# Cross attention of a decoder layer by groups of four heads: scores on row strips, a pass for the maximum and a turned pass

## The chip, the cores and the metric

The kernel runs on one core of one Trainium2 chip. The metric is the time of one execution in device microseconds. The core has a matrix engine (TensorE, PE in the rows; its weight loads are PEld), a vector engine (VectorE, DVE), a scalar engine (ScalarE, ACT), GpSimd (POOL) and a queue that issues the transfers (SyncE, SP). Each takes its instructions in the order in which they are written, and they wait for one another by semaphores.

## What is computed

One decoder layer over 16 batches of 100 rows of width 512, with a context of 722 rows of width 384 for each batch. 16 heads of 32 columns.

```
x = x + self_attention(layernorm(x))            # causal, with rotation of q and k
x = x + cross_attention(layernorm(x), context)
x = x + experts(layernorm(x))                   # 8 experts, two per row, softmax gates

def cross_attention(x, cond):
    q = (x @ q_w + q_b), k, v = split(cond @ kv_w + kv_b)     # 16 heads of 32
    attn = softmax(q k^T / sqrt(32))                          # 100 x 722 a head
    return (attn v) @ proj_w + proj_b
```

## The kernel before

Matrix products run in fp16 with each operand split in a high and a low half: `split3` adds three products (high by high, high by low, low by high).

**Stages.** A prologue transposes and splits the weights. Then `pipeline` runs iterations n = -1 to 16. Iteration n does the cross attention of batch n (`cross`), the preparation of batch n+1 (`prep`: its self attention, and q, k and v of its cross attention) and the output projection of batch n-1 (`tail`, chunks TT and TP). Iterations 1 to 12 are a hardware loop with four in its body; the others are written out. Iteration -1 has only preparation; iteration 15 has no preparation, and does the first tiles of the expert layer's input (chunks FG, FW, FX, FL) instead; iteration 16 has only the tail and the late FX tiles. Then `experts` runs 8 experts over 13 tiles of 128 rows.

**Order.** An iteration has 16 steps, one per head. `STEP_CHUNKS` gives each step its chunks of preparation: X1T and X2T transpose a normalised x, SQ, SK, SV and CQ are products of it, CX0 to CX5 transpose the context, CK0 to CK7 and CV0 to CV5 make keys and values, SS0 to SS3 and SP0 to SP3 are scores and transposed probabilities of self attention, SO and OP its output and projection. The chunks rotate through four PSUM banks; PE makes a chunk, ACT its high half, DVE its low half, and `bank_free` lets chunk c start when chunk c-4 is out. `PE_ORDER = "0SOT123"` is PE's order within a step: the step's first chunk, scores of the next head (S), output of the head before (O), transposes of this head's probabilities (T), the other chunks. `ACT_ORDER` and `DVE_ORDER` do the same for those queues. POOL runs rotation of q and k, the subtraction and scaling of the self attention's softmax, the layer norms and the scaling of the heads, in the order of `pool_iteration`.

**Cross attention of a head.** `pe_scores` (L743) multiplies a stack of q (high, low, high on 96 partitions) by a stack of k (high, high, low): two matmuls of 361 columns give the scores with the 100 rows of x on the partitions. The stacks are made by 24 DMAs an iteration from `split_k` and `split_qk` (L577, L582). `dve_max` takes the maximum over 722 columns (L989) and a bias from it (L992). `act_exp` (L853) writes the exponentials and their sum. `pe_transpose_probs` (L765) transposes them in fp32, six matmuls, `act_probs_high` (L859) copies the high half, `dve_probs_low` (L997) subtracts it. `pe_head_out` (L754) adds 12 matmuls of 64 columns. After four heads DVE joins the halves (`dve_heads_sum`), and once per batch POOL scales by the inverse sums.

Of the kernel before, what the change touches and what calls it, by code (L numbers as in the profile page):

```python
# [21 lines left out]
F32 = mybir.dt.float32  # L22
F16 = mybir.dt.float16
# [4 lines left out]
P = 128  # L28
# [8 lines left out]
CW = 121  # L37
LCP = CT * CW
HC = LC // 2
HP = LCP // 2  # L40
TT = (T + P - 1) // P
# [7 lines left out]
OCOL = 304  # L49
# [9 lines left out]
    ["CX1", "SK"],  # L59
    ["CX2", "CX3", "SV"],  # L60
    ["CX4", "CX5", "TT"],
    ["SS0", "SS1", "TP"],
    ["SS2", "SS3", "CK0"],
    ["CV0", "CK1"],
    ["SP0", "SP1", "CK2"],
    ["SP2", "SP3", "CK3"],
    ["CK4", "SO"],
    ["CK5", "OP"],
    ["CK6", "CK7"],
    ["X2T", "CV1", "CQ"],  # L70
    ["CV2", "CV3"],
    ["CV4"],
# [6 lines left out]
EARLY = 11  # L79
EXTRA_CHUNKS = {  # L80
    B - 1: {0: ["FG0", "FW0"], 1: ["FW1"], 2: ["FW2", "FW3"], **{t + 3: [f"FX{t}"] for t in range(EARLY)},
            15: ["FL0"]},

    -1: {3: ["BV0", "BV1"]},
# [3 lines left out]
PE_ORDER = "0SOT123"  # L88
ACT_ORDER = "0PE123"
# [3 lines left out]
    [f"CX{c}" for c in range(6)] + ["FG0"] + [f"FW{k}" for k in range(KD)] + [f"FX{t}" for t in range(TT)] + [f"CK{c}" for c in range(8)] + [f"CV{c}" for c in range(6)])  # L93


class Iteration:


    def __init__(self, n, odd, cross=True, prep=True, tail=True):
        self.n, self.odd, self.cross, self.prep, self.tail = n, odd, cross, prep, tail  # L100
        self.steps = [[c for c in step if (tail if c in ("TT", "TP") else prep)] for step in STEP_CHUNKS]
# [4 lines left out]

    @staticmethod
    def _count(names):
        return len(names), sum(c in SPLIT for c in names)

    def _before(self, which):
        every = [c for step in STEP_CHUNKS for c in step]
        head = self._count([c for c in every if c not in ("TT", "TP")])[which]
        each = self._count(every)[which]
        prep = head
        head += self._count([c for step in EXTRA_CHUNKS[-1].values() for c in step])[which]
        if isinstance(self.n, int):
            last = ["TT", "TP"] + [c for step in EXTRA_CHUNKS[B - 1].values() for c in step]
            return 0 if self.n < 0 else head if self.n == 0 else (
                head + prep + (min(self.n, B - 1) - 1) * each + (self.n - B + 1 > 0) * self._count(last)[which])  # L120
        return head + prep + (self.n - 1) * each
# [28 lines left out]
def build_layer(nc, x, ctx, sWq, sbq, sWk, sbk, sWv, sbv, sWo, sbo, cWq, cbq, cWkv, cbkv, cWp, cbp,  # L150
                gW, gb, eW, eb, rope, x2_dram, out):
    with ExitStack() as stack:
# [16 lines left out]
        b_rows = sb("b_rows", [6 * KD, P])  # L169
# [6 lines left out]
        x_mid = [sb(f"x_mid{i}", [L, D]) for i in range(2)]  # L176
# [1074 lines left out]
```

## Time and profile before

| what | us |
|---|---|
| three runs | 1566.31, 1567.98, 1581.59; median 1567.98 |
| profiled execution | 1573.9 |
| its span, first to last instruction | 1572.1, mean granted clock 0.955 |
| prologue and iteration -1, up to the first cross scores | 92.6 |
| iterations 0 to 14 | 92.6 to 1175.5 |
| iterations 15 and 16, up to the experts | 89.0 |
| experts | 307.6 |

The page gives the busy time of each engine. The windows view gives it for any stretch, with the granted clock of TensorE. The timeline lists instructions in order of time, runs of equal ones merged: "x12" with one duration is a block of twelve, and the distance from its start to the next row's start is what it takes when the queue is full. A value in brackets is the idle time before, with what ended it.

### The profile page before, as it was taken

How to read it: one execution, taken by the hardware profiler on the slowest of the kernel's cores; microseconds unless marked ns; L12 is line 12 of the kernel's file. 1: busy time of each engine (PE TensorE's matmuls, PEld its weight loads, DVE VectorE, ACT ScalarE, POOL GpSimd, SP SyncE). 2: the span in 40 equal slices, each digit the busy share in tenths (PEclk: the TensorE clock that was granted, in tenths of full speed). 3: DMA queues.
4: the chain of work that ended last, by engine and by line, in shares of the span. 5: the costliest groups of instructions: out<-in, count | busy, mean ns of one | idle time of the engine just before them, and what ended most of it. 6: DMA issues, size and time to landing. Idle time of an engine off the chain costs nothing.

```text
span 1572.1 us, 36339 instructions
## 1 busy us (share of the span) xinstructions
PE 1445.6 (92%) x14004; PEld 1025.8 (65%) x14004; DVE 1069.9 (68%) x1926; ACT 689.2 (44%) x1336; POOL 372.2 (24%) x490
## 2 busy tenths in 40 slices
PE   4889999999989999998999999999996789999999
PEld 4467777777676777776777767677765644444444
DVE  4658878787868687787878686878877554333332
ACT  4336555565646455555556465646554310000000
POOL 1522313133222323141313223232313100000000
PEclk8999999999999999999999999999997589999999
DMA  7133140404132231404040413223133010000002
GB/s 246 28 73 78 28 97 9 99 8 99 40 68 49 57 70 42 94 12 100 8 99 7 99 25 81 49 57 84 28 64 135 1 43 27 28 27 27 28 0 84
DMA packets 82917, 90.38 MB, mean 57 GB/s; under 512 B 32429, under 2 KB 68581, under 8 KB 82749
## 3 DMA queue, kind: packets, MB, share of 16 engines
q1 hardware_dynamic: 82748, 88.05, 23.2%
q8 instruction: 117, 1.92, 0.5%
q14 instruction: 52, 0.42, 0.1%
HBM read 41.06 MB, written 6.55 MB: 30 GB/s over the span
## 4 chain that ended last, share of the span: by engine, by line
PE 64%; DVE 15%; issue 7%; ACT 5%; POOL 4%; SPq 2%; DMA 1%; DVEq 0%; POOLq 0%; ACTq 0%
PE psum L258 43%; PE psum L765 7%; PE psum L743 4%; DVE c_max L989 4%; PE psum L754 3%; DVE s_sum L1051 2%; DVE c_raw L939 2%; ACT prob L853 1%; POOL c_raw L1193 1%; PE psum L697 1%; DVE probT L997 1%; SPq L577 1%; POOL x_norm L1138 1%; PE psum L673 1%; DVE stats L1019 1%
## 5 line engine op out<-in xcount | busy, mean ns | idle before, releaser
L859 ACT ACTIVATE probT<-psum 121x600 f16<-121x600 f32 x256 | 171.8, 671 | 262.1 <-PE psum L765 261.5
L989 DVE TENSOR_REDUCE c_max<-psum 100x1 f32<-100x722 f32 x256 | 231.8, 905 | 78.0 <-PE psum L743 72.6
L853 ACT ACTIVATE prob<-psum,c_bias 100x722 f32<-100x722 f32 x256 | 220.0, 859 | 40.7 <-DVE c_bias L992 40.2
L765 PE MATMUL psum<-ident,prob 100*121 100x100 f32 x1536 | 233.1, 291 | 0.0
L997 DVE TENSOR_TENSOR probT<-psum,probT 121x600 f16<-121x600 f32 x256 | 199.3, 778 | 26.3 <-ACT probT L859 21.5
L258 PE MATMUL psum<-w_kv,cT 128*121 128x512 f16 x864 | 199.4, 379 | 0.0
L765 PEld LDWEIGHTS psum<-ident,prob 100*121 100x121 f32 x1536 | 195.8, 197 | 0.1
L258 PE MATMUL psum<-cT,w_kv 128*128 128x361 f16 x1152 | 195.8, 317 | 0.0
L481 DVE SCALAR_TENSOR_TENSOR w_self_all<-psum,g_now,w_self_all 128x512 f32<-128x512 f32 x104 | 77.8, 751 | 167.5 <-PE psum L258 167.5
L743 PE MATMUL psum<-arena,stack_q 96*100 96x361 f16 x512 | 130.6, 338 | 33.2 <-ACT prob L853 30.3
L258 PEld LDWEIGHTS psum<-w_kv,cT 128*121 128x121 f16 x864 | 112.6, 134 | 59.0
L258 PEld LDWEIGHTS psum<-cT,w_kv 128*128 128x128 f16 x1152 | 110.6, 98 | 57.9
L754 PEld LDWEIGHTS psum<-cv,probT 121*128 121x128 f16 x3072 | 129.7, 100 | 28.5 <-DVE probT L997 3.9
L754 PE MATMUL psum<-cv,probT 121*128 121x64 f16 x3072 | 137.8, 196 | 2.0 <-DVE probT L997 1.6
L258 PE MATMUL psum<-w_cross_q,arena 128*128 128x512 f16 x528 | 118.9, 383 | 1.0 <-DVE w_self_all L481 1.0
L258 PE MATMUL psum<-w_cross_p,arena 128*128 128x512 f16 x528 | 116.1, 379 | 0.0
L848 ACT ACTIVATE cv<-psum 121x512 f16<-121x512 f32 x96 | 57.3, 597 | 106.6 <-PE psum L258 106.2
L839 ACT ACTIVATE split_k<-psum,b_part 128x361 f16<-128x361 f32 x128 | 72.0, 562 | 69.4 <-PE psum L258 68.2
L743 PEld LDWEIGHTS psum<-arena,stack_q 96*100 96x100 f16 x512 | 56.3, 129 | 62.6 <-ACT prob L853 41.4
L1133 POOL TENSOR_SCALAR shift<-moments 100x1 f32<-100x1 f32 x32 | 7.5, 235 | 366.2 <-DVE moments L1021 366.2
L258 PEld LDWEIGHTS psum<-w_cross_q,arena 128*128 128x128 f16 x528 | 51.7, 99 | 64.0 <-issue 5.3
L920 DVE TENSOR_TENSOR cv<-psum,cv 121x512 f16<-121x512 f32 (+1 forms) x98 | 67.6, 690 | 37.5 <-ACT cv L848 33.3
(160 smaller groups left out, 2091.5 us busy)
## 6 DMA issues: line engine op xcount, KB each, us to landing
arena<-split_k SPq DMA_DIRECT2D x192, 180.5 KB, 3.9
c_raw<-in_ctx SPq DMA_DIRECT2D x16, 907.5 KB
stack_q<-split_qk SPq DMA_DIRECT2D x192, 25.0 KB, 1.9
split_k<-in_L_ffn_expert_w SPq DMA_DIRECT2D x4, 1024.0 KB, 5.1
cv<-in_L_ffn_expert_w SPq DMA_DIRECT2D x4, 1024.0 KB, 5.1
x_in<-in_x SPq DMA_DIRECT2D x16, 200.0 KB
x_scratch<-x_mid SPq DMA_DIRECT2D x16, 200.0 KB
w_self_all<-x_scratch SPq DMA_DIRECT2D x12, 256.0 KB, 6.0
```

Of the source, the lines that this page charges most:

```text
L258: last = pe.matmul(out_ap, a(pa), b(pb), start=(i == 0 and j == 0), stop=(i == len(pairs) - 1 and j == 2))
L481: dve.scalar_tensor_tensor(y[:, t], psum[:, (t + odd) % 4, 0:D], g_now[:, odd, t:t + 1], y[:, t], ALU.mult, ALU.add).then_inc(y_done, 1)
L743: last = pe.matmul(score[0:L, hf, 0:HC], stack_q[odd][:, h], stack_k[odd][:, h, hf * HC:(hf + 1) * HC], start=True, stop=True)
L754: last = pe.matmul(pT[:, h % 4 // 2, o:o + 2 * DH], probT_all[:, c:c + P], cv[odd][:, t, h].rearrange("k p d -> k (p d)"), start=t + p == ...
L765: last = pe.transpose(pT[0:CW, t // 3, (t % 3) * L:(t % 3 + 1) * L], prob[h % 2][:, t * CW:(t + 1) * CW], ident[0:L, 0:L])
L839: op = act.activation(split_k[:, 0, i // 2, (i % 2) * HC:(i % 2 + 1) * HC], f[:, 0:HC], ACT.Identity, bias=b_part[:, 3, i // 2:i // 2 + 1])
L848: op = act.activation(cv[not it.odd][:, i, :, 0], f[0:CW, 0:D].rearrange("k (h d) -> k h d", h=H), ACT.Copy)
L853: act.activation(prob[h % 2][:, 0:LC].rearrange("q (a k) -> q a k", a=2), score[0:L, :, 0:HC], ACT.Exp, bias=c_bias[:, int(odd), h:h + 1], ...
L859: act.activation(probT[:, 0].rearrange("k (a c) -> k a c", a=2), pT[0:CW, :, 0:3 * L], ACT.Copy)\
L920: return dve.tensor_tensor(dst, src, high, ALU.subtract)
L989: dve.tensor_reduce(c_max[:, int(odd), h:h + 1], score[0:L, :, 0:HC], AXIS.XY, ALU.max)\
L997: return dve.tensor_tensor(probT[:, 1].rearrange("k (a c) -> k a c", a=2), pT[0:CW, :, 0:3 * L], probT[:, 0].rearrange("k (a c) -> k a c", ...
```

## The change

Four heads (a group, k = 0 to 3) share their steps. c is the step within the group. Head h of a group lives on partitions 32c to 32c+31 of q and k, and these are used where they lie: the stacks and their 24 DMAs are gone.

- `pe_scores(o, hf)`: for one half (361 keys) of a group, three rounds (high by high, high by low, low by high) of four matmuls, one per strip of 32 rows, into banks 0 to 3. DVE takes the maxima of four heads at once (1444 columns), twice per group, and joins the two halves.
- Chunk MX transposes the maxima and splits them in a high and a low half on two rows of each strip.
- `pe_turned_scores(o, part)`: keys on the partitions (128 to a tile, three tiles to a part, two parts), 100 rows of x as columns. Four rounds of four strips for each tile, the fourth a matmul that subtracts the maxima. ACT writes the exponentials of 1200 columns to `prob`, then copies the high half to `prob16`; the low half is subtracted by POOL for groups 0 to 2 and by DVE for group 3. No transposes of probabilities.
- `pe_head_out`: as before, with a column of ones in v that gives the sum; 65 columns. It runs two groups behind.
- The scores use banks 0 to 3 and chunks 4 to 7; each of the four steps of a group fills the same banks 0 to 3 again.
- POOL's list is written out by step; chunks are put on other steps; TP writes to a buffer of its own; the gate weights and rows for the experts are loaded an iteration earlier; three late tiles instead of two.

```diff
-CW = 121
+CW = 128
+PT = 3 * HT * L
 STEP_CHUNKS = [
     ["X1T", "CX0", "SQ"],
...
+    ["CX1", "CX2", "SK"],
+    ["MX0", "CX3", "CX4", "CX5"],
+    ["SV", "CK0"],
+    ["CK1", "SS0", "SS1"],
+    ["CK2", "SS2", "SS3"],
+    ["MX1", "CK3", "CK4"],
+    ["CK5", "CK6"],
+    ["SP0", "SP1", "CV0"],
+    ["SP2", "SP3", "TT", "CV1"],
+    ["SO", "MX2", "TP"],
+    ["OP"],
+    ["CK7", "CV2"],
+    ["X2T", "CV3", "CQ"],
+    ["MX3", "CV4"],
     ["CV5"],
 ]
-EARLY = 11
+EARLY = 10
-    -1: {3: ["BV0", "BV1"]},
+    -1: {6: ["BV0", "BV1"]},
-PE_ORDER = "0SOT123"
-ACT_ORDER = "0PE123"
+PE_ORDER = "0S123"
+ACT_ORDER = "0E1H23"
 DVE_ORDER = "M0L123"
...
+        def pe_scores(pe, n, odd, o, hf):
+            for i, (a, b) in enumerate(((0, 0), (0, 1), (1, 0))):
+                for c in range(HT):
+                    rows = slice(DH * c, DH * (c + 1))
+                    last = pe.matmul(score[0:L, c, 0:HC], cq[odd][rows, a, o],
+                                     split_k[odd][rows, b, o, hf * HC:(hf + 1) * HC], start=i == 0, stop=i == 2)
+            last.then_inc(score_ready, 1)
+        def pe_turned_scores(pe, odd, o, part):
+            for j in range(3):
+                t = 3 * part + j
+                for i, (a, b) in enumerate(((0, 0), (0, 1), (1, 0), (None, None))):
+                    for c in range(HT):
+                        rows = slice(DH * c, DH * (c + 1))
+                        last = pe.matmul(score[:, c, j * L:(j + 1) * L],
+                                         minus[rows] if a is None else split_k[odd][rows, b, o, t * CW:(t + 1) * CW],
+                                         max_split[rows, o % 2] if a is None else cq[odd][rows, a, o],
+                                         start=i == 0, stop=i == 3)
+            last.then_inc(turned_ready, 1)
+        def pe_head_out(pe, n, odd, o, c):
+            if c == 0:
+                if o == GROUPS - 1:
+                    pe.wait_ge(prob_low_last, 2 * n + 2)
+                else:
+                    pe.wait_ge(prob_low, 2 * (GROUPS - 1) * n + 2 * o + 2)
...
+        def pe_cross(pe, it, h):
+            n, k, c = it.n, h // HT, h % HT
+            g = GROUPS * n + k
...
+            if c == 0 and it.cross:
+                pe.wait_ge(max_done, 2 * g + 1)
+            if c == 0 and (begun or (it.cross and k == 3)) and (it.cross or k < 2):
+                pe.wait_ge(heads_summed, g - 2)
+            if c == 1 and it.cross:
+                pe.wait_ge(max_done, 2 * g + 2)
+            if c >= 2 and (begun or (it.cross and k > 0)) and (it.cross or k == 0):
+                pe.wait_ge(exp_done, 2 * g - 3 + c)
+            if k >= 2 and it.cross:
+                pe_head_out(pe, n, it.odd, k - 2, c)
+            elif k < 2 and begun:
+                pe_head_out(pe, n - 1, not it.odd, k + 2, c)
+            if c == 0 and it.cross:
+                pe_scores(pe, n, it.odd, k, 1)
+            elif c in (1, 2):
...
+            elif c == 3:
...
+        def act_exp(act, n, o, part):
...
+            act.activation(prob[:, part].rearrange("k (c q) -> k c q", c=HT), score[:, :, 0:3 * L], ACT.Exp, scale=SOFT)\
+               .then_inc(exp_done, 1)
+        def act_probs_high(act, n, o, part):
...
+            act.activation(prob16[o % 2][:, part * PT:(part + 1) * PT], prob[:, part], ACT.Copy).then_inc(prob_high, 1)
+        def dve_max(dve, n, o, hf):
+            g = GROUPS * n + o
+            dve.wait_ge(score_ready, 2 * g + hf + 1)
+            dve.tensor_reduce(c_most[:, hf], score[0:L, :, 0:HC], AXIS.X, ALU.max).then_inc(max_done, 1)
...
+        def dve_cross(dve, it, h):
+            if c == 0 and it.cross:
+                dve_max(dve, n, k, 1)
+                dve_join_max(dve, n, k)
+            if c == 3:
...
         for what in DVE_ORDER:
             if what == "M":
+                dve_cross(dve, it, h)
             elif what == "L":
+                if h in (2, 3) and begun:
+                    dve_probs_low(dve, n - 1, h - 2)
+                if h in SUM_STEPS and it.prep:
+                    dve_self_sums(dve, m, SUM_STEPS.index(h))
...
         def pool_iteration(pool, it):
+            for h in range(H):
+                if it.prep:
+                    if h == 0 and not (isinstance(n, int) and n < 0):
+                        pool_bias(pool, x_in[:], 2 * m, b_so)
+                    if h in (1, 2):
+                        for part in range(3):
+                            pool_rotate(pool, it, h - 1, part)
+                    if h in (5, 6):
+                        for g in (2 * h - 10, 2 * h - 9):
+                            pool_self_shift(pool, m, g)
+                    if h == 12:
+                        pool_norm(pool, x_mid[not it.odd][:], 2 * m + 1)
+                    if h == 13:
+                        pool_bias(pool, x_mid[not it.odd][:], 2 * m + 1, b_cp)
+                    if h == 14:
+                        pool_split_q(pool, not it.odd, m)
+                    if h == 15 and more:
+                        pool_norm(pool, x_in[:], 2 * m + 2)
+                if h == 8 and begun:
+                    pool_heads_scale(pool, n)
+                if it.cross and h // HT > 0 and h % HT in (2, 3):
+                    pool_probs_low(pool, n, h // HT - 1, h % HT - 2)
+                if it.prep and h in (7, 8):
+                    for g in (2 * h - 14, 2 * h - 13):
+                        pool_self_scale(pool, m, g)
```

## Rows read from the trace of the kernel before

**Rows 1.** The page's first part: busy time, share of the span, instructions.
```profile
PE 1445.6 (92%) x14004; PEld 1025.8 (65%) x14004; DVE 1069.9 (68%) x1926; ACT 689.2 (44%) x1336; POOL 372.2 (24%) x490
```

**Rows 2.** Windows: stretch, length, busy time of each engine, PEclk, DMA share, GB/s.
```profile
162.30:1175.50 1013.20, 954.51 (x10754) 737.02 (x10753) 797.50 (x1442) 563.63 (x1106) 298.66 (x378) 0.98 0.26 56
162.30:233.30 71.00, 67.03 (x770) 51.26 (x769) 57.17 (x104) 40.27 (x79) 21.34 (x27) 1.00 0.27 59
1175.50:1264.50 89.00, 63.74 (x580) 51.93 (x579) 52.55 (x100) 34.14 (x68) 21.68 (x46) 0.64 0.18 62
1264.50:1572.10 307.60, 300.26 (x1432) 141.84 (x1430) 118.84 (x200) 20.23 (x36) 3.56 (x8) 0.99 0.10 34
```

**Rows 3.** PE timeline, iteration end and start: start, us, instruction, [idle before].
```profile
379.55 0.56 PE L630 MATMUL psum<-ident,x_norm 100*128 100x100 f32 x4 [1.56 <-POOL x_norm L1138]
...
382.24 2.31 PE L258 MATMUL psum<-xT,w_self_all 128*128 128x100 f16 x48 [0.46 <-DVE xT L920]
...
384.71 0.47 PE L743 MATMUL psum<-arena,stack_q 96*100 96x361 f16 x2
385.02 0.51 PE L754 MATMUL psum<-cv,probT 121*128 121x64 f16 x12
385.37 0.85 PE L765 MATMUL psum<-ident,prob 100*121 100x100 f32 x6
386.06 1.14 PE L258 MATMUL psum<-xT,w_self_all 128*128 128x100 f16 x22
```

**Rows 4.** PE timeline: a block of 361 columns, then one on row strips.
```profile
331.68 1.55 PE L258 MATMUL psum<-cT,w_kv 128*128 128x361 f16 x9
333.07 2.10 PE L258 MATMUL psum<-w_kv,cT 128*121 128x512 f16 x9
...
395.93 0.76 PE L665 MATMUL psum<-split_qk 32*100 32x100 f16 x24 [0.65 <-DVE cT L920]
396.62 0.36 PE L743 MATMUL psum<-arena,stack_q 96*100 96x361 f16 x1
```

**Rows 5.** Groups by form: shapes, count, busy us, mean ns, idle before.
```profile
L989 DVE TENSOR_REDUCE c_max<-psum 100x1 f32<-100x722 f32 x256 | 231.8, 905 | 78.0 <-PE psum L743 72.6 <-issue 0.8
L853 ACT ACTIVATE prob<-psum,c_bias 100x722 f32<-100x722 f32 x256 | 220.0, 859 | 40.7 <-DVE c_bias L992 40.2
...
L997 DVE TENSOR_TENSOR probT<-psum,probT 121x600 f16<-121x600 f32 x256 | 199.3, 778 | 26.3 <-ACT probT L859 21.5
...
L1051 DVE TENSOR_REDUCE s_sum<-c_raw 100x8 f32<-100x800 f32 x32 | 31.4, 981 | 2.6 <-ACT c_raw L889 2.4
...
L1169 POOL TENSOR_TENSOR split_qk<-tmp_q,split_qk 128x400 f16<-128x400 f32 x16 | 15.1, 946 | 1.3
...
L907 DVE SCALAR_TENSOR_TENSOR w_kv<-cv,w_kv 128x3072 f16<-128x3072 f32 x1 | 3.3, 3348 | 0.0
...
L871 ACT ACTIVATE w_kv<-cv 128x3072 f16<-128x3072 f32 x1 | 2.8, 2767 | 0.0
```

**Rows 6.** Timeline of all engines before X1T: the norm's first step.
```profile
376.11 0.68 DVE L1019 BATCH_NORM_STATS2 stats<-x_in 100x6 f32<-100x512 f32 x1
```

**Rows 7.** Windows: 3 us around a hole and 3 us after.
```profile
304.40:307.40 3.00, 1.49 (x21) 1.23 (x20) 2.44 (x6) 2.07 (x4) 1.79 (x4) 1.00 0.25 46
307.90:310.90 3.00, 3.00 (x24) 2.75 (x23) 1.59 (x3) 0.60 (x2) 0.85 (x1) 0.50 0.12 21
```

**Rows 8.** PE timeline: prologue's end, a back edge, start of the last iteration.
```profile
92.62 0.79 PE L743 MATMUL psum<-arena,stack_q 96*100 96x361 f16 x2 [2.60 <-DMA stack_q<-split_qk]
...
453.58 0.92 PE L630 MATMUL psum<-ident,x_norm 100*128 100x100 f32 x4 [4.50 <-issue]
...
1184.63 0.56 PE L710 MATMUL psum<-ident,x_in 8*128 8x8 f32 x4 [7.62 <-DMA x_in<-in_L_ffn_gate_w]
```

**Rows 9.** POOL timeline: the norms of the late tiles.
```profile
1273.45 0.77 POOL L521 TENSOR_SCALAR w_self_all<-w_self_all,nmean,rstd 128x512 f32<-128x512 f32 x1
...
1275.58 0.77 POOL L521 TENSOR_SCALAR w_self_all<-w_self_all,nmean,rstd 128x512 f32<-128x512 f32 x1
```

More of the change, by code:

```diff
@@ L100, in __init__ @@
         self.n, self.odd, self.cross, self.prep, self.tail = n, odd, cross, prep, tail
-        self.steps = [[c for c in step if (tail if c in ("TT", "TP") else prep)] for step in STEP_CHUNKS]
+        self.steps = [[c for c in step if self._has(c)] for step in STEP_CHUNKS]
         if isinstance(n, int):
@@ L105, in __init__, with _has, _count @@
         self.order = [c for step in self.steps for c in step]
+    def _has(self, name):
+        return self.tail if name in ("TT", "TP") else self.cross if name[:2] == "MX" else self.prep
     @staticmethod
-    def _count(names):
-        return len(names), sum(c in SPLIT for c in names)
+    def _count(names, which):
+        return sum(c in SPLIT for c in names) if which else len(names)
     def _before(self, which):
         every = [c for step in STEP_CHUNKS for c in step]
[L113 to L116, printed above, removed]
+        late = self._count([c for c in every if c in ("TT", "TP")], which)
+        first = self._count([c for step in EXTRA_CHUNKS[-1].values() for c in step], which)
+        first += self._count([c for c in every if c not in ("TT", "TP") and c[:2] != "MX"], which)
+        each = self._count(every, which)
         if isinstance(self.n, int):
[L118 to L121, printed above, removed]
+            last = self._count([c for c in every if c in ("TT", "TP") or c[:2] == "MX"], which)
+            last += self._count([c for step in EXTRA_CHUNKS[B - 1].values() for c in step], which)
+            return 0 if self.n < 0 else first if self.n == 0 else (
+                first + each - late + (min(self.n, B - 1) - 1) * each + (self.n - B + 1 > 0) * last)
+        return first - late + self.n * each
     def bank(self, chunk):
@@ L183, in build_layer @@
         split_qk = sb("split_qk", [P, 4, KD, L], F16)
[L184 removed]
+        cq_all = sb("cq", [P, 2, 2, KD, L], F16)
+        cq = [cq_all[:, i] for i in range(2)]
         sv = sb("sv", [L, H, 2, DH], F16)
@@ L1171, in pool_iteration @@
-            if isinstance(n, int) and n < 0:
-                pool.wait_ge(chunk_out, it.done("BV1"))
-                pool_bias(pool, x_in[:], 0, b_so)
-            if begun:
-                pool.wait_ge(c_rinv_done, n)
-                pool.wait_ge(pT_out, H * n + 1) if it.cross else pool.wait_ge(c_summed, 1)
-                heads = c_out[:].rearrange("q (h d) -> q h d", h=H)
-                pool.tensor_tensor(heads, heads, c_rinv[:].unsqueeze(2).to_broadcast([L, H, DH]), ALU.mult)\
-                    .then_inc(c_out_done, 1)
```

510 lines of the change are left out of this document (257 added, 253 removed).

## The prediction

> **What bounds the kernel now.** I read the page's first part: TensorE (PE) is busy 92% of the span, VectorE (DVE) 68%, GpSimd (POOL) 24% [rows 1]. Then the windows by stage [rows 2]. The program is a prologue up to the first scores at 92.6 us, sixteen iterations (each: cross attention of one batch, preparation of the next), then the expert layer. The 14 iterations n=1 to 14 take 1013.2 us, 72.4 each, PE busy over 94% of them; iteration 1, at clock 1.00, takes 71.0. The last iteration with what follows it takes 89.0 us at a granted clock of 0.64, and the experts 307.6. The PE timeline shows the price of one head: scores 0.31 us, head output 0.35, transposes 0.69 from start to start [rows 3]. Adding up such starts for a whole iteration gives 65.5 us of issue and some 5.5 of holes (4.0 by the busy record; a last matmul's tail of about 0.2 us hides the rest). The largest hole is where X1T waits for the layer norm, 1.56 us, and SQ for xT, 0.46 [rows 3]. So the loop is bound by PE, and what matters is PE's work and its holes.
>
> **PE's work per iteration.** Removed: 16 x (0.31 + 0.35 + 0.69) = 21.6 us. Added:
> - Head outputs stay, 65 columns instead of 64: 16 x 0.36 = 5.8.
> - Maximum pass: 8 half passes (two per group of four heads), each 12 matmuls of 361 columns on four row strips. The block of 24 matmuls of 100 columns on two strips takes 0.69 us from its start to the next [rows 4], where 24 one behind another, 100 columns each at 2.4 GHz, would need 1.0. So strips run side by side: the starts within the block are about 47 ns apart a round, and 0.13 us is lost at the block's ends. A 361-column matmul is 0.155 us (nine in 1.39 [rows 4]); three rounds and the ends give 0.60 (bounds: 0.60, or 12 x 0.155 = 1.9 if strips took turns). Times 8: 4.8.
> - Turned pass: 8 parts of 12 rounds of 100 columns: 0.56 + 0.13 = 0.69. The stationary has 128 columns; the block has 100. I take 0.75. Upper bound: the head output's 128-column loads come every 29 ns, and four in turn make a round 116 ns and a part 1.52. Times 8: 6.0.
> - MX, four transposes: 0.5.
>
> Sum 17.1, so 4.5 us less per iteration. The 24 stack DMAs go; in the loop PE is seldom late for them.
>
> The Trainium skill ("TensorE: Matmul & The Clock Gate", Measured speedup vs the span model) gives 3.07 times for four row tiles rather than nearly 4; an estimate by it is 0.61 us for a half pass before its ends and 0.7 for a part, some 2 us more per iteration, or 30 us in all. No run here shows four row strips; the two-strip block speaks for the larger gain.
>
> **The new passes as a chain.** Scores of a half, or of a turned part, fill banks 0 to 3, and each step of PE waits until the previous filling was read: by a DVE maximum over 1444 columns (722 take 0.905 and 800 take 0.981, 1.03 ns a column: 1.65 us), or by an ACT exponential over 1200 (1.18, from 0.859 at 722 and the copies of 3072 in 2.77) [rows 5]. Then ACT copies the high half (1.18), and the low half is subtracted: for groups 0 to 2 on POOL (400 columns take 0.946, so 1200 take 2.0 if a third of that was fixed cost and 2.8 if none; I take 2.5), for group 3 on DVE (3072 take 3.35: 1.40) [rows 5]. DVE loses 16 x (0.905 + 0.778) and 16 bias products, and gains 8 x 1.65, 2 x 1.4 and small ones: about 10 us less, ACT 8 less, POOL 15 more (21.3 to 37). None is full. But they are late. I walked one iteration in the order of the four queues, with these durations and 0.05 to 0.2 us from engine to engine. Holes of PE:
> - *Step 0, 6.4 us.* The stats of x_in follow CV4 on DVE; 3.44 us after their start X1T may run [rows 3, 6], 1.9 us after step 15's scores ended. At step 15 POOL runs this norm before the low half of group 2, part 1: 2.5 us more, and PE's first head output of step 0 waits for that (`prob_low`). Then output and scores 0.96, then DVE, whose order puts the maximum (0.2 + 1.65), the join 0.15 and only then X1T's low half 0.57: SQ starts 8.1 us after step 15's scores, and PE has 1.65 us of work for that time. Before: 2.0 us of hole.
> - *Step 4, 1.6.* Output of group 3 waits for the second DVE low half, which stands behind maximum, head sum and SV.
> - *Steps 5 and 6, 0.6.* DVE is full from step 3 to 6.
> - *Step 8, 2.4.* SP0 waits for POOL: shifts of groups 2 and 3 (their maxima late by the DVE queue), two low halves (5.0), then the scaling 0.85.
> - *Step 12, 0.5; step 13, 1.6* (X2T after OP, which stands behind a DVE maximum).
>
> Sum 13.1, against 5.5: +7.6. Without the clock an iteration is 71.0 - 4.5 + 7.6 = 74.1.
>
> **The clock.** The stretch in which PE was busy half the time is followed by one at 0.50, its lower level 1.2 GHz [rows 7]. Over the 14 iterations that and the back edges of the loop (a gap of 4.5 us that the profile puts to issue, once in four iterations [rows 8]) cost 72.4 - 71.0 = 1.4 each. The hole at step 0 (20% busy over 8 us) should bring it down in every iteration, with some 5 us of PE's work inside the slow time: 2.6. So +1.2; the back edges stay. What a slow stay costs at step 8 as well (another 1) I leave to the range. Loop: 14 x (3.1 + 1.2) = +60.
>
> **Ends.** Prologue: PE waits 2.60 us for the stacks before the first scores [rows 8]; with the bias products moved behind CK work I take -4 (bounds -1 and -6). Iteration 0 has no outputs and no turned part in steps 0 to 3, nor a late low half: -3. Last iteration: PE waits 7.62 us for the gate weights at its start [rows 8], which now land an iteration earlier. Against that, each group is a serial chain of two maxima and two exponentials with PE's work at half clock between them, 14 to 16 us against 17.7 for four heads, and group 3 has its turned pass, low half and outputs still to do in the next iteration, some 16 us. Together about 82 against 89: -7 (bounds -25, +5). Experts: three late tiles instead of two; one costs POOL 2.1 us, and PE waits on it [rows 9]: +2.5.
>
> Sum: +60 - 4 - 3 - 7 + 2.5 = +48. The profiled execution took 1573.9 (span 1572.1 and 1.8 around it) and would become 1622; the median shown is 1568.0, so 1616.
>
> **Rivals.**
> 1. *PE stays the bound; the holes don't open* (faster). DVE, ACT and POOL all have room on average (68%, 44%, 24%), and if the low half of group 2 and the scaling are ready in time, the 4.5 us are saved: 14 x -4.5 - 11 = -74, 1494; half of the holes gives about 1530. It decides at the `prob_low` wait: it holds if the POOL subtraction takes well under 1.5 us, or H of step 14 and the subtraction end before the stats. Against it: POOL's 0.946 us for 400 columns hardly varies. 18%.
> 2. *No net change.* Consecutive DVE rows overlap by up to 0.09 us and POOL's 1200 columns may take 2.0; holes 10 instead of 13, clock as before: 14 x 0.1 - 11, 1558, with some loss of clock 1570. 15%.
> 3. *Holes as worked out, clock as before*: 14 x 3.1 - 11.5 = +32, 1600. 12%.
> 4. *The strips don't run side by side in the turned pass*, because 128-column loads take turns: 1.52 a part, +6 an iteration, 5 of it seen: 1616 + 70 = 1686. 10%.
>
> **How the numbers follow.** The forecast (the holes and the clock) has 45%, with 1590 to 1645 as its own range. Slower by over 1% (about what a measurement of this kernel tells from no change): cases 3, 4 and the forecast, 0.67. Within 1%: 0.15. Faster: 0.18. The range 1545 to 1680 takes in case 2, half of the road to case 1, and most of case 4.
>
> **What would show it.** Right: PE busy below 86% in the loop; X1T to SQ over 5 us in each iteration, with POOL's low half of 1200 columns (about 2.5 us) as the releaser at step 0; clock 0.95 or less over the loop; SP0 waiting for the POOL scaling; c_most 1.65 us and the exponential 1.18; the block of a half pass 0.6 and a turned part 0.7 to 0.8 from start to start; the loop at 75 to 78 us an iteration. Wrong: iterations of 68 to 70 us; low halves done before X1T; a turned part of 1.5.

## The result and the profile after

The changed kernel takes 1629.69 us (median of four runs, 1628.57 to 1631.01); the kernel before, beside it, 1571.51. The ratio is 1.035, 95% interval 1.031 to 1.040: slower, by 58 us, where 1616 and 48 were predicted. The span of the profiled execution is 1628.7 us, 56.6 more than before.

The page's first part, to be read against [rows 1]:

```profile
PE 1412.9 (87%) x19700; PEld 919.9 (56%) x19700; DVE 907.5 (56%) x1495; ACT 607.6 (37%) x888; POOL 621.8 (38%) x610
```

PE, DVE and ACT all do less; only POOL does more. PE's busy time fell by 32.7 us and its idle time grew from 126.5 to 215.8. So the time went into waits. The windows by stage (columns as in [rows 2]: the 14 iterations; a stretch within one of them; the last iteration; the experts):

```profile
153.80:1231.40 1077.60, 932.39 (x15739) 649.27 (x15736) 655.34 (x1062) 490.70 (x715) 516.74 (x463) 0.93 0.07 23
620.10:630.30 10.20, 7.50 (x81) 6.40 (x82) 3.33 (x5) 0.49 (x1) 2.22 (x2) 0.50 0.01 2
1231.40:1318.90 87.50, 56.86 (x1084) 44.22 (x1082) 43.22 (x75) 33.15 (x42) 37.56 (x49) 0.65 0.09 28
1318.90:1628.70 309.80, 301.56 (x1448) 142.65 (x1446) 120.24 (x203) 20.80 (x37) 5.35 (x12) 0.99 0.10 34
```

The loop went from 1013.2 to 1077.6 us, 76.97 an iteration, at a clock of 0.93 instead of 0.98. The prologue ends at 85.0 (92.6 before), iteration 0 takes 68.8 (69.7), the last 87.5 (89.0), the experts 309.8 (307.6). The differences are -7.6, -0.9, +64.4, -1.5 and +2.2, together the 56.6 of the span.

Where an iteration loses it, on PE's timeline (one iteration, from 616 us; the brackets hold the idle time before the row and its releaser):

```profile
616.25 0.67 PE L742 MATMUL psum<-arena,cq 32*100 32x361 f16 x12
618.72 0.56 PE L627 MATMUL psum<-ident,x_norm 100*128 100x100 f32 x4 [1.80 <-POOL x_norm L1204]
621.15 0.84 PE L770 MATMUL psum<-cv,arena 128*128 128x65 f16 x12 [1.86 <-POOL arena L1256]
621.92 1.15 PE L742 MATMUL psum<-arena,cq 32*100 32x361 f16 x12
623.00 0.90 PE L699 MATMUL psum<-ident,c_raw 128*128 128x128 f32 x3
625.55 4.18 PE L273 MATMUL psum<-xT,w_self_all 128*128 128x100 f16 x48 [1.66 <-DVE xT L971]
...
643.91 0.53 PE L770 MATMUL psum<-cv,arena 128*128 128x65 f16 x12 [1.30 <-DVE arena L1062]
...
658.96 0.55 PE L670 MATMUL psum<-ident,c_raw 100*100 100x100 f32 x4 [1.72 <-POOL c_raw L1243]
...
677.62 0.54 PE L770 MATMUL psum<-cv,arena 128*128 128x65 f16 x12 [0.88 <-DVE c_rinv L1071]
...
681.62 0.53 PE L627 MATMUL psum<-ident,x_norm 100*128 100x100 f32 x4 [0.82 <-POOL x_norm L1204]
```

From step 15's scores (616.25) to the self projection (625.55) pass 9.3 us, three waits included, one behind the other: for the norm, for the low half, for xT. Four smaller ones follow at steps 4, 8, 12 and 13. The two engines that PE waits for, in the same stretch; first POOL:

```profile
617.90 0.77 POOL L1204 TENSOR_SCALAR x_norm<-x_in,shift,rstd 100x512 f32<-100x512 f32 x1 [0.22 <-POOL rstd L1202]
618.63 2.46 POOL L1256 TENSOR_TENSOR arena<-prob,arena 128x1200 f16<-128x1200 f32 x1
```

then DVE:

```profile
623.12 1.66 DVE L1050 TENSOR_REDUCE c_most<-psum 100x4 f32<-100x1444 f32 x1 [3.49 <-PE psum L742]
624.82 0.17 DVE L1055 TENSOR_TENSOR c_max<-c_most 100x8 f32<-100x8 f32 x1
624.92 0.57 DVE L971 TENSOR_TENSOR xT<-psum,xT 128x400 f16<-128x400 f32 x1
```

POOL runs norm and low half back to back, and PE's head output waits for the second. DVE stood idle for 3.49 us with nothing but its own queue's order between it and xT's addition: the maximum stands ahead, and its scores come after the head output. That the window from 620.10 to 630.30 shows a clock of 0.50 (1.2 GHz) is the second half of the price: the output takes 0.77 us from start to start there, and 0.46 at full clock. In all 14 iterations of the loop the self projection behind the third wait takes 3.6 to 4.0 us from start to start, where the same 48 matmuls take 2.14 from 631.71 on.

PE's waits over the whole span, largest first (us in total, times, longest):

```profile
PE psum L627 <- POOL x_norm L1204: 35.1, 29, 1.9
PE psum L273 <- DVE xT L971: 27.3, 17, 1.7
PE psum L770 <- POOL arena L1256: 27.2, 16, 1.9
PE psum L670 <- POOL c_raw L1243: 26.7, 17, 2.4
PE psum L770 <- DVE arena L1062: 23.6, 16, 4.0
```

Before, the largest was PE's wait for ACT's exponential, 30.3 us in all, and the one for x_norm was 22.1. The new long operations by group (count, busy, mean ns, idle before):

```profile
L1050 DVE TENSOR_REDUCE c_most<-psum 100x4 f32<-100x1444 f32 x128 | 212.5, 1660 | 147.6 <-PE psum L742 147.5
L1256 POOL TENSOR_TENSOR arena<-prob,arena 128x1200 f16<-128x1200 f32 x96 | 235.9, 2464 | 122.6 <-ACT arena L906 122.6
...
L898 ACT ACTIVATE prob<-psum 128x1200 f32<-128x1200 f32 x128 | 149.7, 1170 | 86.8 <-PE psum L753 86.6
...
L906 ACT ACTIVATE arena<-prob 128x1200 f16<-128x1200 f32 x128 | 154.0, 1203 | 1.7
```

1.66, 2.46, 1.17 and 1.20 us, where 1.65, 2.5, 1.18 and 1.18 were scaled from [rows 5]. And what the strips cost on PE, from start to start in a full-clock stretch:

```profile
649.35 0.54 PE L770 MATMUL psum<-cv,arena 128*128 128x65 f16 x12
649.82 0.31 PE L753 MATMUL psum<-cq,arena 32*128 32x100 f16 x12
...
650.46 4.33 PE L273 MATMUL psum<-cT,w_kv 128*128 128x361 f16 x27
654.63 0.53 PE L770 MATMUL psum<-cv,arena 128*128 128x65 f16 x12
655.08 0.67 PE L742 MATMUL psum<-arena,cq 32*100 32x361 f16 x12
655.68 1.55 PE L273 MATMUL psum<-cT,w_kv 128*128 128x361 f16 x9
```

A half pass is 0.60 (655.08 to 655.68), as predicted; a turned part 0.64 (0.75 predicted); a head output 0.46 (0.36).

### The profile page after: what moved, and what is told of

The parts are those of the page before. It is cut to its first block, busy times and chain, and to the rows that moved or that the text cites. A ratio compares the mean times of both kernels' runs of the same rounds, so it can differ in the third digit from the quotient of the medians.

```text
span 1628.7 us, 46374 instructions
## 1 busy us (share of the span) xinstructions
PE 1412.9 (87%) x19700; PEld 919.9 (56%) x19700; DVE 907.5 (56%) x1495; ACT 607.6 (37%) x888; POOL 621.8 (38%) x610
## 4 chain that ended last, share of the span: by engine, by line
PE 54%; POOL 18%; issue 14%; DVE 10%; ACT 2%; DMA 1%; SPq 0%; POOLq 0%; DVEq 0%; ACTq 0%
PE psum L273 38%; POOL arena L1256 7%; PE psum L770 4%; PE psum L753 3%; PE psum L742 3%; DVE c_most L1050 2%; POOL c_raw L1237 2%; PE psum L670 2%; POOL split_qk L1226 2%; POOL tmp_k L1229 2%; POOL split_qk L1232 1%; DVE stats L1078 1%; POOL rstd L1202 1%; POOL x_norm L1204 1%; DMA arena<-in_L_attn_Wv 1%
## 5 line engine op out<-in xcount | busy, mean ns | idle before, releaser
L1050 DVE TENSOR_REDUCE c_most<-psum 100x4 f32<-100x1444 f32 x128 | 212.5, 1660 | 147.6 <-PE psum L742 147.5
L1256 POOL TENSOR_TENSOR arena<-prob,arena 128x1200 f16<-128x1200 f32 x96 | 235.9, 2464 | 122.6 <-ACT arena L906 122.6
L770 PE MATMUL psum<-cv,arena 128*128 128x65 f16 (+1 forms) x3072 | 145.6, 200 | 78.0 <-POOL arena L1256 27.2
L273 PE MATMUL psum<-w_kv,cT 128*128 128x512 f16 (+1 forms) x864 | 210.6, 394 | 0.0
L770 PEld LDWEIGHTS psum<-cv,arena 128*128 128x128 f16 (+1 forms) x3072 | 129.3, 102 | 111.0 <-issue 45.4
L898 ACT ACTIVATE prob<-psum 128x1200 f32<-128x1200 f32 x128 | 149.7, 1170 | 86.8 <-PE psum L753 86.6
L906 ACT ACTIVATE arena<-prob 128x1200 f16<-128x1200 f32 x128 | 154.0, 1203 | 1.7
L273 PEld LDWEIGHTS psum<-w_kv,cT 128*128 128x128 f16 (+1 forms) x864 | 86.4, 105 | 94.8 <-issue 17.1
L273 PE MATMUL psum<-xT,w_self_all 128*128 128x100 f16 x1536 | 101.0, 243 | 25.9 <-DVE xT L971 25.9
L273 PEld LDWEIGHTS psum<-xT,w_self_all 128*128 128x128 f16 x1536 | 97.1, 119 | 32.3 <-DVE xT L971 32.1
L742 PE MATMUL psum<-arena,cq 32*100 32x361 f16 x1536 | 93.6, 350 | 0.0
```

Source lines behind the costliest of these rows:

```text
L273: last = pe.matmul(out_ap, a(pa), b(pb), start=(i == 0 and j == 0), stop=(i == len(pairs) - 1 and j == 2))
L742: last = pe.matmul(score[0:L, c, 0:HC], cq[odd][rows, a, o], split_k[odd][rows, b, o, hf * HC:(hf + 1) * HC], start=i == 0, stop=i == 2)
L770: last = pe.matmul(head_out[:, c], prob16[o % 2][0:r, at:at + P], cv[odd][0:r, t, HT * o + c, 0:HV], start=t + p == 0, stop=t + p == CT)
L898: act.activation(prob[:, part].rearrange("k (c q) -> k c q", c=HT), score[:, :, 0:3 * L], ACT.Exp, scale=SOFT)\
L906: act.activation(prob16[o % 2][:, part * PT:(part + 1) * PT], prob[:, part], ACT.Copy).then_inc(prob_high, 1)
L1050: dve.tensor_reduce(c_most[:, hf], score[0:L, :, 0:HC], AXIS.X, ALU.max).then_inc(max_done, 1)
```

## The experiments

All start from the changed kernel, except the last, which starts from the kernel before. Where nothing else is said a version ran two to six times. The kernel before ran beside each, with medians between 1571.9 and 1576.7; ratios are to it.

### The order on DVE at step 0

```
-                for what in DVE_ORDER:
+                for what in ("0ML123" if h == 0 and it.prep else DVE_ORDER):
```

> At step 0 DVE takes X1T's low half before the maximum of the second half pass; nothing else is changed. Theory A (the iteration is long because three queues meet at step 0, each in a fixed order): SQ no longer waits for xT, the hole of 1.66 us plus a tail of 0.2 goes in each of 15 iterations, about -28 us, and up to -45 with less time at the lower clock: 1585 to 1602. Rival B (PE's own work on the strips and the changes between full rows and strips make it long, and the hole would be filled by another wait): within 6 us of 1629.7. Rival C (only the clock matters): the hole goes but the granted clock stays at 0.93, and less than 10 us is saved.

Measured: 1597.44 us, ratio 1.013 (1.003 to 1.024), 32 us below the changed kernel. These are two runs only, 1590.98 and 1603.91; the trace is of the longer one, 26 us below. The wait for xT is gone from PE's list, the others are where they were (27.2 for the low half, 26.7 for the scaling), and the loop takes 1055.1 us instead of 1077.6. The price of that one place in DVE's queue was 1.6 us an iteration in the loop, and 4.0 in iteration 0. The clock of the loop stayed at 0.93, so it falls with the two waits ahead alone.

### The order of norm and low half on POOL

```
-                    if h == 15 and more:
-                        pool_norm(pool, x_in[:], 2 * m + 2)
 ...
                     pool_probs_low(pool, n, h // HT - 1, h % HT - 2)
+                if h == 15 and more:
+                    pool_norm(pool, x_in[:], 2 * m + 2)
```

> At step 15 POOL runs the low half of group 2, part 1, before the norm of x_in. Theory A: the wait of PE's first head output for POOL (1.86 us) goes, but X1T comes 2 to 2.4 us later, so SQ starts at the same time: 1624 to 1636. Rival D (the subtraction on POOL is the cost, and the norm in front of it only delays it): -1.9 x 15 = -28 us, 1601.

Measured: 1632.32 us, ratio 1.036 (1.030 to 1.041). PE's waits of this kernel:

```profile
PE psum L627 <- POOL x_norm L1204: 65.7, 31, 3.9
PE psum L273 <- DVE xT L971: 27.6, 17, 2.0
```

The 27.2 us for the low half are gone, and those for the norm grew by 30.6. The hole only moved one instruction forward. What bounds step 0 is the sum of the two on POOL, not which is first.

### Transposes to keep the clock up

The transposes of X1T and of CX0 are issued six times in place, with the same results: 35 more transposes an iteration.

```
-                for k in range(KD):
+                for k in list(range(KD)) * (6 if name == "X1T" and it.cross else 1):
 ...
-                for j in range(3):
+                for j in list(range(3)) * (6 if i == 0 and it.cross else 1):
```

> X1T's four transposes and CX0's three are done six times over in the same places, 20 + 15 more transposes an iteration, about 1.8 + 1.6 us of PE work at the full clock inside the second and third hole of step 0; the results are the same. Theory A with the clock: no wait gets longer, PE is busy there, the granted clock over the loop rises from 0.93 to 0.97 or more and the 3.9 us an iteration that the slow time costs shrink by half or more: -25 to -50 us, 1580 to 1605. Rival B (PE bound): 3.4 x 15 = +51, 1680. If the holes set the pace and the clock does not matter: within 8 us of 1629.7.

Measured: 1599.84 us, ratio 1.015 (1.012 to 1.018), 30 us less though PE does more. Windows of this kernel, the loop and the 10 us behind the start of a self projection:

```profile
151.10:1198.80 1047.70, 945.82 (x16234) 674.65 (x16231) 656.61 (x1062) 490.79 (x715) 517.05 (x463) 0.98 0.08 24
...
610.10:620.10 10.00, 9.96 (x240) 8.97 (x241) 5.58 (x8) 6.10 (x9) 5.86 (x5) 1.00 0.01 3
```

The chain of step 0 is not shorter: step 15's scores start at 600.35 and the self projection at 610.14, 9.8 us against 9.3. But the projection then runs at a clock of 1.00, and the iterations are 2.1 us shorter (1047.7 against 1077.6, over 14). So the fall of the clock that the holes bring cost at least 2.1 + 0.5 us an iteration, the 2.6 of the prediction. Theory A's range is met, and that PE's own work bounds the loop is refuted.

### The scaling ahead of a low half at step 7

```
+                if it.prep and h == 7:
+                    for g in (0, 1):
+                        pool_self_scale(pool, m, g)
                 if it.cross and h // HT > 0 and h % HT in (2, 3):
                     pool_probs_low(pool, n, h // HT - 1, h % HT - 2)
-                if it.prep and h in (7, 8):
-                    for g in (2 * h - 14, 2 * h - 13):
+                if it.prep and h == 8:
+                    for g in (2, 3):
```

> At step 7 POOL scales groups 0 and 1 of the self attention before the low half of group 0, part 1, instead of after it. Theory A: SP0's wait of 1.72 us nearly goes, the head output of step 8 may wait up to 0.5 for the low half that is now 1.7 us later: -1.2 to -1.9 an iteration, -18 to -30 us, 1600 to 1612. Rival E (DVE is full from step 3 to 8, and what POOL gains is late on DVE): within 8 us of 1629.7.

Measured: 1649.78 us, ratio 1.047 (1.042 to 1.051): 20 us slower, where 18 to 30 less were expected. A miss. POOL's and PE's timelines of this kernel (POOL first):

```profile
736.39 2.47 POOL L1256 TENSOR_TENSOR arena<-prob,arena 128x1200 f16<-128x1200 f32 x1
738.82 1.67 POOL L1243 TENSOR_TENSOR c_raw<-c_raw,s_rinv 100x400 f32<-100x400 f32 x2
740.44 2.46 POOL L1256 TENSOR_TENSOR arena<-prob,arena 128x1200 f16<-128x1200 f32 x1
```

```profile
742.96 0.54 PE L770 MATMUL psum<-cv,arena 128*128 128x65 f16 x12 [2.20 <-POOL arena L1256]
```

The scaling is done at 740.5 and its wait of 1.72 us is gone. But step 8's head output waits for the later low half, which now ends at 742.9, and that wait is 2.20. In the changed kernel both consumers stood right behind the same POOL run of 4.9 + 1.66 us; I had taken the low half for one with room. It is the second experiment's result again, 0.5 us worse. The loop's clock fell to 0.91, so the remainder of the 1.4 us an iteration is likely the clock's; that was not tested by itself.

### The next sequence's norm a step earlier

The norm moves from step 15 to step 14, right behind the split of the queries, and its statistics from step 14 to 13.

```
                         pool_split_q(pool, not it.odd, m)
-                    if h == 15 and more:
-                        pool_norm(pool, x_in[:], 2 * m + 2)
+                        if more:
+                            pool_norm(pool, x_in[:], 2 * m + 2)
 ...
-                if h == H - 2 and it.prep and not (isinstance(n, int) and n == B - 2):
+                if h == H - 3 and it.prep and not (isinstance(n, int) and n == B - 2):
```

> The next sequence's statistics are taken at step 13 and its normalisation runs on POOL at step 14, right behind the split of the queries, so that step 15's POOL work is the low half alone. Theory A (step 0 is held twice: POOL's chain statistics, norm 0.77 us, low half 2.46 us, and behind it DVE's maximum): the wait of the first transposes for x_norm (35.1 us in all, 1.8 an iteration) is gone or moves to step 14, and the wait of step 0's head output for the low half (27.2 us in 16 waits, 1.86) shrinks by about 1.5 to 2 us an iteration, since the low half no longer stands behind the norm and its four small instructions; the wait of the self projection on xT stays only where the maximum still stands ahead of it. That is 2 to 3 us an iteration of holes and some clock: 1570 to 1605. Rival (the low half is held by ACT's high copy, not by the norm): the head output's wait stays at 1.8 and only the first transposes' goes; as step 0's later work then waits longer, the time is 1620 to 1632.

Measured: 1610.99 us, ratio 1.026 (1.020 to 1.033), 19 us less than the changed kernel but short of the range. The first transposes wait no more, yet the head output's wait grew to 3.1 instead of shrinking. POOL's timeline of this kernel says why:

```profile
602.52 0.77 POOL L1204 TENSOR_SCALAR x_norm<-x_in,shift,rstd 100x512 f32<-100x512 f32 x1 [0.22 <-POOL rstd L1202]
603.25 4.87 POOL L1256 TENSOR_TENSOR arena<-prob,arena 128x1200 f16<-128x1200 f32 x2
```

Both low halves now stand behind the norm, since the norm was put ahead of step 14's. Neither theory had that.

### Both moves

> Both moves: statistics and norm a step earlier, and DVE's chunk additions ahead of the maximum at step 0. Theory A (the order on POOL and DVE at the iteration's end is the price of the change, and what it leaves is the four waits in the middle): from the last half pass of a sequence to the start of the self projection 4.0 to 5.0 us instead of 9.3, iterations of 71 to 74 us, 1550 to 1585, which is the kernel before within its uncertainty. Rival (the two gains are the same hole counted twice): no more than the DVE move alone, 1590 to 1604. Rival (PE's own work and the clock's stays set the loop): the holes go but iterations stay over 75 us.

Measured: 1582.28 us (12 runs), ratio 1.006 (1.003 to 1.009). From step 15's scores to the self projection pass 6.8 us (592.02 to 598.82) instead of 9.3, where 4 to 5 were expected, since the low halves' 3.1 us are still there. Iterations take 74.3 on average. The two gains add up almost fully: 32 and 19 apart, 47 together.

This trace also gives the price of the clock by itself. Two neighbouring iterations, each from one self projection to the next, have the same waits to within 0.1 us each:

```profile
526.96:598.82 71.86, 63.89 (x1125) 44.49 (x1124) 46.92 (x77) 35.05 (x51) 36.89 (x33) 0.97 0.07 23
598.82:673.94 75.12, 67.02 (x1125) 46.63 (x1124) 46.94 (x77) 35.12 (x51) 36.90 (x33) 0.93 0.07 22
```

The one at the lower clock is 3.3 us longer, and PE's busy time in it 3.1. The loop's other iterations without a back edge fall in the same two kinds, 71.9 to 72.2 us and 74.3 to 75.3.

### One of each block twice

```
-            for i, (a, b) in enumerate(((0, 0), (0, 1), (1, 0))):
+            for i, (a, b) in list(enumerate(((0, 0), (0, 1), (1, 0)))) * (2 - hf):
 ...
-            for j in range(3):
+            for j in list(range(3)) * (1 + part):
 ...
-            for t in range(CT):
+            for t in list(range(CT)) * (2 if c == 1 else 1):
```

> In each group of four heads one head output (step 1 of the group), one turned part (step 2) and one half pass of the scores (step 3) are issued twice in place, with the same results. It prices TensorE's change between full rows and strips: theory (a change costs about 0.1 us each way, and a head output with strips behind it pays for one, a block of strips with full rows behind it for the other): the second output adds 0.34 to 0.37 us to the 0.46 from its first start to the strips, the second half pass 0.45 to 0.47 to 0.60, the second turned part 0.50 to 0.54 to 0.64. Rival (the instructions themselves are that slow, no change costs anything): each doubling doubles the stretch, +0.46, +0.60 and +0.64. Total added work by the theory 4 x (0.36 + 0.46 + 0.52) = 5.4 us an iteration, of which the holes take back some where they follow: 1680 to 1715.

Measured: 1680.37 us, ratio 1.068 (1.060 to 1.076). PE's timeline of this kernel: the doubled output, a single output and the doubled half pass, a doubled turned part:

```profile
648.18 0.89 PE L770 MATMUL psum<-cv,arena 128*128 128x65 f16 x24
649.01 0.31 PE L753 MATMUL psum<-cq,arena 32*128 32x100 f16 x12
...
657.47 0.53 PE L770 MATMUL psum<-cv,arena 128*128 128x65 f16 x12
657.93 1.13 PE L742 MATMUL psum<-arena,cq 32*100 32x361 f16 x24
658.99 2.94 PE L273 MATMUL psum<-cT,w_kv 128*128 128x361 f16 x18
...
669.51 0.31 PE L753 MATMUL psum<-cq,arena 32*128 32x100 f16 x12
...
670.68 4.33 PE L273 MATMUL psum<-cT,w_kv 128*128 128x361 f16 x27
```

The second output adds 0.83 - 0.46 = 0.37 us, the second half pass 1.06 - 0.60 = 0.46, the second turned part 1.17 - 0.64 = 0.53, all within the theory's windows and below the rival's. The 0.09, 0.14 and 0.11 that are missing stand once per block; each of the three blocks ends where PE goes from full rows to strips or back. Four matmuls of 361 columns on four strips take 0.46 / 3 = 0.153 us together, the time of one ([rows 4]: 0.155): the strips run fully side by side. The added 5.4 us of work lengthened an iteration by 3.1 (80.1 against 77.0); the clock, 0.943 over the span instead of 0.924, and shorter waits gave the rest back.

### POOL's first low half into its idle time

The trace of the kernel with both moves shows POOL idle for 5.5 us ahead of the split of the queries at step 14, with the first high half done 1.4 us before the split can start.

```
                     if h == 14:
+                        if it.cross:
+                            pool_probs_low(pool, n, 2, 0)
                         wait_alone(pool, chunk_out, it.done("CQ"))
 ...
-                if it.cross and h // HT > 0 and h % HT in (2, 3):
+                if it.cross and h // HT > 0 and h % HT in (2, 3) and not (h == 14 and it.prep):
                     pool_probs_low(pool, n, h // HT - 1, h % HT - 2)
```

> The two moves of before (statistics and norm a step earlier, DVE's additions ahead of the maximum), and POOL takes the first low half of group 2 ahead of the split of the queries at step 14, where it was idle for 5.5 us, instead of behind the norm at the iteration's end. Theory A (what is left at step 0 is POOL's run of norm and two low halves, 591.34 to 596.2 in that kernel): the high half is ready 1.4 us before the split's operands, so the last low half ends 1.3 us earlier; the head output's wait at step 0 falls from 3.1 us to 1.5 to 1.9, iterations by 1.3 us or more with the clock: 1550 to 1570. Rival (the split comes 1.1 us later and the scores of the next sequence wait for it): a new wait of about 1 us at step 15, the time as in the kernel with the two moves, 1575 to 1585.

Measured: 1555.18 us, ratio 0.9885 (0.985 to 0.992). The first version of the change that beats the kernel before.

### The context's transposes into the hole

```
-                for what in PE_ORDER:
+                for what in ("01S23" if h == 0 and it.prep else PE_ORDER):
```

> As the run with the low half first, and at step 0 the context's transposes (0.7 us, on nothing's account late) go ahead of the head output into the hole, instead of behind the scores. Theory: PE spends 0.7 us of the hole on work it has anyway, so the iteration is up to 0.7 us shorter than in the run with the low half first, 1540 to 1562. Rival (the end of the hole is not what bounds there, since the self projection waits for xT): no change, within 5 us of that run.

Measured: 1532.23 us, ratio 0.973 (0.970 to 0.976), 23 us below the run with the low half first, where at most 15 were expected. (These are medians of six; the runs of the version with the low half first spread from 1548 to 1564, the new ones from 1530 to 1536.) The windows behind step 0's head output tell the rest, first of the run with the low half first:

```profile
579.60:584.20 4.60, 4.60 (x64) 4.13 (x63) 2.73 (x4) 0.49 (x1) 0.68 (x1) 0.63 0.00 0
```

then of this one, with the whole iteration and the loop:

```profile
575.30:579.90 4.60, 4.60 (x130) 4.16 (x130) 3.67 (x6) 0.76 (x2) 1.65 (x2) 1.00 0.02 4
```

```profile
571.80:640.70 68.90, 62.41 (x1127) 43.46 (x1124) 46.85 (x76) 34.97 (x52) 36.88 (x34) 1.00 0.08 24
148.30:1131.60 983.30, 886.92 (x15743) 615.76 (x15740) 655.82 (x1062) 489.90 (x715) 515.94 (x460) 0.98 0.08 26
```

Both have PE always busy. The 48 matmuls of the self projection take 3.28 us from start to start in the first (from 580.98) and 2.15 in the second (from 575.84). Moving 0.7 us of work into the hole left a hole of 1.48 instead of 1.79, and in this iteration the clock no longer fell. The direct gain is at most 14 x 0.7 = 10 us. It is likely less: where both kernels keep the full clock, the way from step 15's scores to the self projection is 4.41 us with the low half first (288.42 to 292.83) and 4.04 here (571.80 to 575.84), 0.4 an iteration. The rest is the clock's. An undisturbed iteration takes 68.9 us, 2.1 less than the 71.0 of [rows 2].

### Filling, with and without the context ahead

> As the run with the low half first, and the x_norm transposes at step 0 are issued four times in place (12 more of 0.14 us, 1.7 us an iteration, same results), as much as the hole that is left there. Theory (the hole at step 0 is also what lets the granted clock fall, and the fall costs more than the hole): the loop's clock is 0.96 or more, against 0.94, and the time 10 to 25 us below the run with the low half first, though PE does more. Rival (the four waits further on, 1.30, 1.73, 0.88 and 0.82 us, are enough to let the clock fall): the clock and the time stay, within 5 us.

Measured: 1535.18 us, ratio 0.974 (0.971 to 0.978), 20 us below the run with the low half first, and the loop's clock is 0.98. Work for nothing gives as much as moved work, so it is the clock that was bought.

> As the run with the context's transposes ahead, and the x_norm transposes three times in place (8 more, 1.1 us an iteration, in the hole of 1.5 us that is left at step 0). Clock theory: the loop's clock there is 0.98 already and its undisturbed iterations run at 1.00, so the filling has nothing to give back: within 6 us of 1532. Rival (any hole at step 0 costs clock beyond its length, in the longer iterations of 74 to 77 us too): 5 to 15 us below 1532.

Measured: 1532.40 us, ratio 0.9735 (0.969 to 0.978), no change. Once the clock holds, filling gives nothing. The iterations of 74 to 77 us that are left stand at the loop's back edges, which were there before too [rows 8]; a few others take 69.8 to 70.7.

### The kernel before with its statistics earlier

```
-                if h == H - 2 and it.prep and not (isinstance(n, int) and n == B - 2):
+                if h == H - 3 and it.prep and not (isinstance(n, int) and n == B - 2):
```

> The kernel before the change, and in it alone the move of the next sequence's statistics from step 14 to step 13 on DVE (its normalisation on POOL comes right behind the split of the queries there already). It asks how much of what the reordered kernels gain is to be had without the change. Theory (the reorderings pay back holes that the change had made): in the old kernel only its one wait of 1.56 us for x_norm can go, 1.0 to 1.5 us an iteration and little clock, as the loop's clock is 0.98: 1548 to 1565, above the best reordered kernel (1532) by 15 us or more. Rival (the reordering is the whole gain, and the change itself costs even then): 1530 or below.

Measured: 1560.22 us (12 runs), ratio 0.992 (0.989 to 0.995): some 13 us are to be had without the change, and the reordered changed kernel stands 28 us below that. Of the 2.7% that it gains on the kernel before, 0.8% are to be had without the change. Its loop:

```profile
162.70:1169.40 1006.70, 946.88 (x10753) 729.11 (x10752) 797.20 (x1440) 562.26 (x1106) 296.81 (x374) 0.99 0.26 57
```

PE's busy time in the loop is 946.9 us here and 886.9 in the reordered kernel. That is the change's own gain, and it can only be collected where the waits don't eat it.

## Why the prediction was right, and where its sizes were off

The mechanism was the predicted one: less work on PE, eaten by holes at step 0 and at four places after it, and by the clock. The forecast put an iteration of the loop at 72.4 + 4.3 = 76.7 us; it takes 76.97. By its steps:

- *PE's work*: 17.1 predicted, 16 x 0.455 + 8 x 0.60 + 8 x 0.64 + 0.5 = 17.7 measured. The head output was the mis-sized term, +1.5: I took the 0.35 of [rows 3], where full rows came before and after it, and left out the change to strips (0.09 in the doubled blocks). The turned part was set too high, -0.9. The Trainium skill's 3.07 times ("TensorE: Matmul & The Clock Gate", Measured speedup vs the span model) does not show inside a block; the doubled half pass gives 4 x 0.155 / 0.153, about 4 times. A single half pass with its ends comes to 12 x 0.155 / 0.60 = 3.1 times.
- *Step 0*: the chain was put at 8.1 us from the end of step 15's scores to the self projection. With 0.60 for these scores it is 625.55 - 616.85 = 8.7. The order of its links was right. Head output and scores inside it were costed at full clock, 0.96; at 0.50 they take 1.85 (621.15 to 623.00). In two iterations they ran at full clock (1.11 us, 697.63 to 698.74), and there the chain is 0.75 us shorter, 7.95. So the fall of the clock lengthens the very chain that causes it, and the sum had the clock only behind it. As holes, 6.4 were predicted; 5.3 are recorded, and three tails of 0.2.
- *The other holes*: step 4, 1.30 for 1.6; steps 5 and 6, 0.30 for 0.6; the scaling, 1.72 for 2.4; step 12, 0.88 for 0.5; step 13, 0.82 for 1.6. Together 5.0 for 6.7: the walk made the later queues too late. That offset the terms that were too small, PE's work and the clock.
- *The clock*: 2.6 us an iteration predicted; the filled kernel shows at least 2.6, the two neighbouring iterations with both moves 3.3 for one that is slow against one that hardly is, and the balance leaves more than 2.6 too. PE's work is 65.5 - 21.6 + 17.7 = 61.6 us, the recorded waits (those above, with one of 0.30 at step 6) are 10.3, some 0.2 of tail at each of eight waits makes 1.6; of the 76.97, 3.4 remain for clock and back edges. How they share it is an estimate.
- *Ends*: prologue -7.6 for -4 (beyond the bound of -6; besides the 2.60 us for the stacks, a wait of 4.2 for `w_cross_p` on DVE is gone, which the prediction didn't name), iteration 0 -0.9 for -3, last iteration -1.5 for -7, experts +2.2 for +2.5. In the last iteration the gate weights' 7.62 us are gone as predicted; the groups of four that follow stand 16.7 us apart (half passes at 1267.55 and 1284.23), where 14 to 16 was worked out, with PE's outputs waiting for exponentials, maxima and low halves in turn.
- *Against the rivals*: that PE stays the bound fell with the profile (10.3 us of waits) and again with the filled kernel, where more PE work took less time. That the clock stays as before fell with 0.93. That the strips take turns fell with 0.64. The point named for the first rival, the wait on `prob_low`, was among those that decided: with that wait shortened and the norm's and DVE's order mended, the reordered kernel gains 2.7% on the kernel before.
- *Signs that missed*: PE is busy 86.5% of the loop, where below 86% was named, and a turned part takes 0.64, where 0.7 to 0.8 was.

The total was closer than its terms. 48 against 56.6 (the difference of the spans) hides errors of both signs: +4.4 in the loop, -3.6 in the prologue, +2.1 and +5.5 at iteration 0 and the end. Inside the loop it was the same: PE's work +0.6 an iteration, the holes with their tails 11.9 for 13.1, the clock and back edges some +0.8. That these nearly cancel is luck.

## What to carry to other kernels

When a change takes work from the bound engine and gives long operations to others, don't ask whether those have room on average; write down, for the place where one iteration hands over to the next, the exact order of each queue, and look for the short operation that now stands behind a long one. Swapping two operations on one engine whose consumers both wait gains nothing or loses (two trials here); moving one into that engine's idle time does (27 us). And where the clock falls with a hole, count it inside the chain as well, and try moving real work into the hole before judging the change: 0.7 us of transposes gave 23 us in all.

## What had not been expected of the hardware

- A change between full rows and row strips costs PE 0.09 to 0.14 us a block (the second output, turned part and half pass in place cost 0.37, 0.53 and 0.46 us, the first 0.46, 0.64 and 0.60). The Trainium skill ("TensorEngine Tiling (Array Packing)", Key Properties) says that changing the tiling mode drains the engine, without a price; the trace agrees.
- Four row strips of 32 rows give nearly the full factor of four in a steady stream, for 361 columns (0.153 us a round, one full-row matmul 0.155) and for 100 (0.53 / 12 = 0.044 us a round, one full-row matmul 2.14 / 48 = 0.045).
- Equal holes can have very different prices. In the kernel with the low half first, behind a hole of 1.79 to 1.80 us at step 0, the self projection took 3.28 us in one iteration (from 580.98) and 2.13 in another (from 292.83). With 0.7 us of transposes moved ahead of the hole, which was then 1.48, it took 2.14 to 2.15 in 12 of the loop's 14 iterations. So one hole in one iteration doesn't show what a hole costs.
